# Attention: who copies the third quarter of the turned probabilities in every second head

## What is computed

```python
# B = 4, queries and keys 512 each, 32 heads of 16 dimensions
q = apply_axial_rope((x @ Wq).reshape(b, n, 32, 16), pos_map)
k = apply_axial_rope(k, ctx_pos_map)
logits = jnp.einsum('bqhd,bkhd->bhqk', q, k) * scale
w = jax.nn.softmax(logits, axis=-1)
attn = jnp.einsum('bhqk,bkhd->bqhd', w, v)
return attn.reshape(b, n, 512) @ Wout + bout
```

## Time and profile before

| | |
|---|---|
| median of 3 runs | 5672.06 us (5664.07 to 5676.34) |
| profiled execution | 5684.37 us, its span 5682.7 us |
| busy over the span | PE 85%, VectorE 68%, ScalarE 51%, GpSimd 41% |
| attention stage | about 4736 to 5375 us after the span's start |
| exponents L2927 | 512 instructions, 346.1 us, 686 ns each |
| maxima L2893 | 512 instructions, 327.8 us, 682 ns each |
| transposes L2853 | 2048 instructions, 275.6 us, 278 ns each, overlapping |
| VectorE's copies L2911 | 256 instructions, 177.1 us, 692 ns each |

### The profile page before, as it was taken

One profiled execution on the slowest core, in us unless ns is written; L12 is line 12 of the kernel. 1 busy time (PEld: TensorE's weight loads), 2 busy tenths in 40 slices (PEclk: granted clock), 3 DMA queues, 4 the chain that ended last, 5 costly groups with the idle time before them and its releaser, 6 DMA issues. The chain is left out here.

```text
span 5682.7 us, 81944 instructions
## 1 busy us (share of the span) xinstructions
PE 4824.2 (85%) x24459; PEld 3104.9 (55%) x24459; DVE 3843.3 (68%) x6409; ACT 2875.2 (51%) x5207; POOL 2330.1 (41%) x3008
## 2 busy tenths in 40 slices
PE   6899758999568999989999899999999786888767
PEld 4566535555336666666666666666666443444433
DVE  5777673222357777777777777777777386888767
ACT  5666361111035655555556555555555325777633
POOL 3466410110225545545555454554545145444300
PEclk8999878999778999999999999999999898999989
DMA  2111005244431111121111211111111023222200
GB/s 65 31 31 31 15 30 210 91 138 158 142 105 52 45 47 43 44 61 52 45 43 51 59 48 46 41 49 50 48 46 40 14 77 88 54 55 54 92 13 26
DMA packets 360251, 345.35 MB, mean 61 GB/s; under 512 B 125313, under 2 KB 257921, under 8 KB 358625
## 3 DMA queue, kind: packets, MB, share of 16 engines
q1 hardware_dynamic: 315200, 269.94, 16.0%
q0 software_dynamic: 44704, 71.14, 4.0%
HBM read 264.76 MB, written 75.89 MB: 60 GB/s over the span
## 5 line engine op out<-in xcount | busy, mean ns | idle before, releaser
L1939 POOL TENSOR_TENSOR delta_rule_suffix<-delta_rule_suffix,delta_rule_prefix 128x256 f32<-128x256 f32 x448 | 498.3, 1112 | 1080.6 <-ACT delta_rule_prefix L2035 828.9
L2316 PE MATMUL delta_rule_level<-delta_rule_qk_second,delta_rule_k_first 128*128 128x128 f32 x3072 | 440.7, 289 | 111.6 <-DVE delta_rule_L_small L2127 104.6
L2316 PEld LDWEIGHTS delta_rule_level<-delta_rule_qk_second,delta_rule_k_first 128*128 128x128 f32 x3072 | 395.0, 199 | 163.3 <-DVE delta_rule_qk_second L2138 115.8
L2292 PE MATMUL delta_rule_proj<-delta_rule_hT,delta_rule_w_qkv 128*128 128x512 f32 x1024 | 466.5, 599 | 0.0
L312 POOL TENSOR_TENSOR scan_hc<-scan_hs,scan_c_rows 128x512 f32<-128x512 f32 x256 | 337.7, 1328 | 235.3 <-DVE scan_hs L479 221.5
L479 DVE TENSOR_TENSOR_SCAN scan_hs<-scan_decay,scan_inp 128x512 f32<-128x512 f32 x256 | 306.2, 1215 | 151.1 <-PE scan_inp L541 82.1
L2138 DVE TENSOR_TENSOR delta_rule_qk_second<-delta_rule_qk,delta_rule_prefix 128x512 f32<-128x512 f32 x448 | 370.7, 827 | 47.9 <-issue 12.8
L2196 DVE TENSOR_TENSOR delta_rule_prefix<-delta_rule_prefix 128x256 f32<-128x256 f32 x448 | 306.1, 683 | 131.2 <-PE delta_rule_level L2304 72.8
L2809 POOL DMA_DIRECT2D attend_k_stack<-parts_dram x384 | 229.3, 599 | 348.9 <-PE attend_scores L2845 314.5
L1930 POOL TENSOR_TENSOR delta_rule_k_first<-delta_rule_qk,delta_rule_suffix 128x256 f32<-128x256 f32 x384 | 304.5, 793 | 160.2 <-PE delta_rule_level L2304 107.5
L2143 DVE SCALAR_TENSOR_TENSOR delta_rule_qk<-delta_rule_proj,delta_rule_conv_w,delta_rule_qk 128x511 f32<-128x511 f32 (+2 forms) x384 | 287.5, 749 | 121.8 <-ACT delta_rule_qk L2014 102.1
(11 more groups left out here) (479 smaller groups left out, 11378.5 us busy)
## 6 DMA issues: line engine op xcount, KB each, us to landing
moe_w_d<-in_w_down SPq DMA_DIRECT2D x39, 512.0 KB, 4.2
scan_c_rows<-bc_dram SPq DMA_DIRECT2D x64, 256.0 KB, 3.8
delta_rule_w_qkv<-in_kda_wq SPq DMA_DIRECT2D x64, 256.0 KB
delta_rule_w_qkv<-in_kda_wk SPq DMA_DIRECT2D x64, 256.0 KB
delta_rule_w_qkv<-in_kda_wv SPq DMA_DIRECT2D x64, 256.0 KB
delta_rule_inv_beta<-beta_dram SPq DMA_DIRECT2D x64, 256.0 KB, 4.1
delta_rule_w_o<-in_kda_wo SPq DMA_DIRECT2D x64, 256.0 KB, 5.0
small_dram<-delta_rule_L_small SPq DMA_DIRECT2D x64, 256.0 KB, 2.0
```

What stands on the lines that cost most here:

```text
L1939: pool.tensor_tensor(first, first, whole_second, ALU.mult).then_inc(suffix_done, 1)
L2292: last = pe.matmul(to, w_qkv[p][:, i, k, :], hT[:, b % 2, k, :], start=(k == 0), stop=(k == DT - 1))
L2316: last = pe.matmul(level_ps[(i + 1) % 2][:, c, :], left, qk_second[:, i % 2, :, c * CHUNK // 2:(c + 1) * CHUNK // 2], start=True, stop=True)
```

## The change

In heads with an odd j the copy of i = 2 goes from ScalarE to VectorE, and ScalarE keeps the copy of i = 0 alone. It reads buffer 0 as before, and counts up the same semaphore. VectorE's list in odd heads is then: maximum 0, maximum 1, copy 1, maximum 2, copy 2, maximum 3, copy 3, sums; ScalarE's is copy 0, exponents 0 to 3. Even heads stay as they were.

```diff
+        def vector_copies(j, i):
+
+            return i % 2 == 1 or (i == 2 and j % 2 == 1)
+
...
@@ VectorE, step
-                        if i % 2 == 1:
+                        if vector_copies(j, i):
                             dve.wait_ge(probs_turned, TPB * m + i + 1)
                             if i == 1:
                                 dve.wait_ge(weighed, 2 * n + j // GROUP + 1)
-                            dve.tensor_copy(probsT[:, j, i, :], turned[1][:].rearrange("p a b -> p (a b)")).then_inc(odd_copied, 1)
+                            dve.tensor_copy(probsT[:, j, i, :], turned[i % 2][:].rearrange("p a b -> p (a b)")).then_inc(
+                                (even_copied, odd_copied)[i % 2], 1)
...
@@ ScalarE, step
-                        if i % 2 == 0:
+                        if not vector_copies(j, i):
                             act.wait_ge(probs_turned, TPB * m + i + 1)
```

## The result

| | median | range | executions |
|---|---|---|---|
| before | 5672.06 us | 5662.84 to 5676.34 | 5 |
| changed | 5704.82 us | 5695.90 to 5717.86 | 5 |

The ratio is 1.0058, with a 95% interval from 1.0038 to 1.0077: slower by 33 us, where 10.4 were forecast. It lies outside the range given (5671 to 5696). So the first question is whether the loop lost more than worked out, or something outside it did.

The account below looks back on a forecast made before the run. Bound: the loop of TensorE's transposes, ScalarE's copy 2, exponents 2 and 3, no engine being full. 61 odd heads x 0.17 = 10.4 us, stall at the stage's end unchanged: 5672.1 + 10.4 = 5682.4 us, range 5671 to 5696.

Parts of the forecast that it names:

- The circle: Attention loop: TensorE's transposes of quarter 2, ScalarE's copy 2, exponents 2 and 3, back to TensorE; 4.87 us a head.
- The price, 0.17 us per odd head: Odd heads: maximum 3 stands behind the waiting copy 2 on VectorE, so exponent 3 starts 0.17 us later.
- pieces 0.61 and 0.71: Odd heads: 0.61 us from copy 2's start to maximum 3's, then 0.71 us to exponent 3's.
- rival B: Odd heads: exponent 3's wait is dearer, 0.25 us each, 15 us in all, 5687; chance 0.13.
- 61 heads, 10.4 us: Attention stage: 64 odd heads without two in the first tile and the very last, 61 x 0.17 = 10.4 us.
- The first tile's heads 1 and 3: No weighing there, so copy 2 could start earlier and exponent 3 stays where it is: cost zero.
- the output copy's cover: After head 3 of a tile: copy 1 comes 0.25 us late, exponent 2 has 0.5 room; without it 4 us.
- Rival A: Odd heads: ScalarE's relief arrives, exponent 3 moves 0.67 us earlier, 61 heads win about 41 us, 5631; chance 0.04.
- The stall at the end: End of attention stage: a sums copy takes 9.09 us beside GpSimd's bias adds, costing 7.4; no change assumed.
- the shift between adds and copies: Odd heads' sums copies move 0.78 us against the bias adds; which is caught may change: +9, +4, -1 or -7.4.
- The sum: Whole kernel: the loop's 10.4 us added to the median of three timed runs, 5672.1, giving 5682.4 us, +0.18%.

## Why the prediction was wrong, point by point

- **The circle** (TensorE's transposes of quarter 2, copy 2, exponents 2 and 3): right. Copy 2 stayed at 2.02 after copy 0, whoever made it.
- **The price, 0.17 us per odd head**: right, 5.04 against 4.87, in all four traces of the changed kernel; pieces 0.61 and 0.71 as taken. The dearer handover of rival B (0.25) didn't occur.
- **61 heads, 10.4 us**: right; the one-layer kernels show it unmixed (629.2 - 618.8). In the whole kernel, from the first fourth exponent to the last the traces show 9.6 us more (636.0 and 626.4), in which the head with the stall is 0.6 shorter (11.5 against 12.1). The first tile's heads 1 and 3 lost nothing (4.65 and 4.67 against 4.68), and the output copy's cover held.
- **Rival A, ScalarE's relief**: right to give it little as the diff stands, and its 0.67 was real: it came to 0.69 as soon as maximum 3 stood ahead.
- **The stall at the end**: that it may change or go was right, and so, roughly, was its price of 7.4: the head that has it lasts 12.1 instead of 4.9 (7.2 more), and the stages of the two traces of before are 8.3 apart. I read the shift between adds and copies as what decides; the repetitions show both outcomes at the same place. That the stall stood in both of the first two traces, and so all but fell out of their difference (0.6), was luck. In the whole kernel all four traces of the changed kernel had it and two of three with the old order. That may be why 12.9 us is the mean difference and not 10, though 2.4 of standard error explains that too; seven traces don't settle it.
- **The step that failed** is the one in "The sum": "The change in the loop is a constant per head, so it goes onto the median: 5672.1 + 10.4". It has no term for the 4,736 us ahead of the stage, as if they took the same in every execution: the median of three runs, spread over 12 us, was taken as the kernel's level, and the range was built on "the runs' own spread". Ninety later executions of the kernel before lie between 5640.9 and 5700.7, and most of that comes from ahead of the stage: in twelve traces of kernels that are equal up to there it began anywhere from 4714.5 to 4758.0 (standard deviation 11.3), while what follows it took 306.7 to 309.6 in all of them. 22.3 of the 33.5 us between the first two traces arose there, with 43 us more of TensorE's lower clock level; what brings that on stays open. The 11.3 us that I took for telling a change from none is less than one execution's standard deviation.
- **So the forecast of the median missed**, that of the loop didn't: +10.4 predicted; the long comparison says +12.9 with 2.4 of standard error, the kernel cut to one layer +9.1 between the four executions before and the lower two of the changed one.

## What to carry to other kernels

An engine works off its list in order, so before giving it a step, look at what it will wait for and what is queued behind: a copy on the idler engine cost time because a maximum stood behind it, and with the same copy one place later the stage was 40 us shorter than before. Busy shares said nothing here, neither for nor against.
Where a change is worth 0.2% of a kernel, cut the kernel to the layer that holds it: there the executions of the kernel before lay within 2.2 us of each other (the changed one's in two groups 7.6 apart), and its two traces gave the 10.4 us of the loop to a tenth; thirty-six executions of 5,690 us gave 13 with a standard error of 2.4. And look at the granted clock of each execution beside its time.

## What the runs showed of the hardware that I had not expected

- VectorE's 128x4 copy within SBUF beside a row of GpSimd adds with two inputs in SBUF was let in between two adds (0.45, 0.49, 0.54 us for 0.16) or shut out through eight of them (9.09 us), at the same point of the same program. With the adds one to a tile it took at most 0.56 us in the kernel before. The Trainium skill ("SBUF — State Buffer", Who interferes with whom) has the loser wait for the instruction that holds the ports; here it waited for the end of the whole row. VectorE's 128x512 copies out of PSUM took 0.67 to 0.69 throughout.
- The steady loop repeats from execution to execution, its median heads 4.87 and 5.04 us in every trace of the kernels before and changed, while executions of the kernel before as a whole differ by up to 60 us. The loop runs at a granted clock of 1.00; the stages ahead of it, at 0.93 to 0.94 on the mean, are where the scatter is.
